# Six of eight pairs of x tiles loaded a second time in transposed form, with the order of the loads around them changed

## The reference, cut to what matters

```
c0 = agg_w(cond) @ x + agg_b(cond)                    # per batch a 64x64 mix of the channels
logits = c0 @ gate_w ; top 2 of 8 experts ; softmax   # gate_w is 1024 x 8
x1 = x + sum over the 2 experts of  w_e * (c0 @ expert_w[e])
c1 = grouped convolution of x1 along the row + context
out = x1 + c1 @ weight.T + rank-16 terms of 2 of 8 experts
```

## Time and profile before

| | |
|---|---|
| median of 3 runs | 867.15 us (867.11 to 867.46) |
| the profiled execution's own time | 865.47 us |
| its span | 863.6 us |
| TensorE busy in the span | 820.6 us (95%) |
| VectorE, ScalarE busy | 400.2 us, 222.9 us |
| queue q1, all loads and stores issued by SP | 90.27 MB, 32.3% of 16 engines' span |
| `res<-in_x` on q1 | 16 transfers of 512 KB, median 14.6 us to landing |
| `work<-in_x_t` on q1 | 3 transfers of 1024 KB, median 7.1 us to landing |
| `c_scratch<-work` on q1 | 16 transfers of 512 KB, median 5.4 us to landing |

### The profile page before, as it was taken

How to read it: one execution, slowest core, us unless ns; L and a number is a source line. 1 busy time by engine, 2 the same in 40 slices (tenths; PEclk the granted TensorE clock), 3 DMA queues, 4 the chain that set the end, 5 groups by cost and what they waited for, 6 DMA issues and landing times.

```text
span 863.6 us, 13175 instructions
## 1 busy us (share of the span) xinstructions
PE 820.6 (95%) x4308; PEld 677.2 (78%) x4309; DVE 400.2 (46%) x920; ACT 222.9 (26%) x347; POOL 89.1 (10%) x137
## 2 busy tenths in 40 slices
PE   5988779999999999999999999999999999999985
PEld 3645468888888888888887888888898889889863
DVE  1376753142333313333133051466666656656597
ACT  2445333242333413333233152310010010001100
POOL 1000021011111011111011012122112111100000
PEclk9999879999999999999999999999999999999999
DMA  8667559656371824727246243684644653521048
GB/s 282 243 198 244 193 203 395 271 178 208 109 268 69 283 97 134 242 81 284 84 164 212 97 167 93 209 251 129 153 108 106 157 125 97 142 77 25 1 133 256
DMA packets 61220, 146.11 MB, mean 169 GB/s; under 512 B 6880, under 2 KB 23536, under 8 KB 60656
## 3 DMA queue, kind: packets, MB, share of 16 engines
q1 hardware_dynamic: 40528, 90.27, 32.3%
q0 software_dynamic: 9968, 36.19, 14.3%
q10 hardware_dynamic: 10704, 19.41, 6.0%
HBM read 97.60 MB, written 39.85 MB: 159 GB/s over the span
## 4 chain that ended last, share of the span: by engine, by line
PE 82%; DMA 7%; DVE 6%; issue 2%; ACT 2%; SPq 1%; DVEq 0%; ACTq 0%; POOL 0%; POOLq 0%
PE bank L1283 62%; PE bank L1322 6%; PE bank L1274 4%; PE bank L1331 4%; DMA c_scratch<-work 2%; PE bank L1182 1%; PE bank L1385 1%; DVE work L1117 1%; PE bank L1145 1%; DMA work<-in_expert_w 1%; PE bank L1230 1%; DMA res<-in_x 1%; DMA work<-y_scratch,pos_c 1%; PE bank L1159 1%; DMA x1p<-res 1%
## 5 line engine op out<-in xcount | busy, mean ns | idle before, releaser
L1283 PE MATMUL bank<-weights,l_hi 128*128 128x512 f32 x1696 | 524.3, 390 | 0.0
L1283 PEld LDWEIGHTS bank<-weights,l_hi 128*128 128x128 f32 x1696 | 319.6, 188 | 64.6
L1283 PE MATMUL bank<-weights,l_lo 128*128 128x512 f32 x848 | 336.2, 396 | 1.4 <-DVE l_lo L906 1.3
L1283 PEld LDWEIGHTS bank<-weights,l_lo 128*128 128x128 f32 x848 | 159.9, 189 | 34.1 <-issue 2.9
L906 DVE TENSOR_TENSOR l_lo<-bank,l_hi 128x512 fp32r<-128x512 f32 x37 | 25.6, 692 | 184.1 <-ACT l_hi L684 184.1
L938 DVE TENSOR_TENSOR weights<-work,weights 128x1024 fp32r<-128x1024 f32 x64 | 76.2, 1223 | 51.7 <-ACT weights L695 51.2
L695 ACT ACTIVATE weights<-work 128x1024 fp32r<-128x1024 f32 x64 | 65.2, 1055 | 43.2 <-DMA work<-in_expert_w 25.1
L540 POOL DMA_INDIRECT work<-c_scratch,idx x37 | 39.9, 1079 | 200.4 <-PE bank L1274 199.3
L1322 PE MATMUL bank<-conv_sb,x1p 128*128 128x128 f32 x512 | 59.8, 275 | 0.6 <-DMA x1p<-res 0.6
L1322 PEld LDWEIGHTS bank<-conv_sb,x1p 128*128 128x128 f32 x512 | 58.8, 192 | 0.9 <-DMA x1p<-res 0.8
L735 ACT ACTIVATE l_hi<-work 128x512 fp32r<-128x512 f32 x32 | 18.4, 623 | 158.1 <-PE bank L1283 157.3
(11 more groups left out here) (174 smaller groups left out, 530.9 us busy)
## 6 DMA issues: line engine op xcount, KB each, us to landing
work<-in_expert_w SPq DMA_DIRECT2D x68, 512.0 KB, 6.4
y_scratch<-work ACTq DMA_DIRECT2D x74, 256.0 KB, 2.1
res<-in_x SPq DMA_DIRECT2D x16, 512.0 KB, 14.6
c_scratch<-work SPq DMA_DIRECT2D x16, 512.0 KB, 5.4
out<-work SPq DMA_DIRECT2D x16, 512.0 KB, 4.2
res<-in_x_ph SPq DMA_DIRECT2D x14, 512.0 KB, 5.5
x1p<-res SPq DMA_DIRECT2D x112, 64.0 KB, 4.7
y_scratch<-ca SPq DMA_DIRECT2D x7, 512.0 KB, 10.1
```

The source lines that it names most:

```text
L1283: mm = pe.matmul(to[:, :], a[:, k, :], b[:, k, cols * HALF:(cols + 1) * HALF], start=(k == 0 and n == 0), stop=(k == HC - 1 and n == 2))
```

## The change

`LOADED` becomes the pairs 2 to 7, so only pairs 0 and 1 are still transposed on the chip, and `x_t` in memory grows from three to six pairs (the host lays it out; no arithmetic). The count of landed `x_t` loads is kept in two semaphores, one for even and one for odd pairs. The four loads of `kern` go behind tile 1. The piece `raw0` that SP asks for at the end of pair `it` is now `it + 1` and waits for `rest0(it - 1)`, where it was `it + 2` and `rest0(it)`. For the last pair, TensorE does `logits` between the first two `mix` products, and `lists(6)` ahead of `ranks(7)`; VectorE does `one_hot(6)` ahead of `route(7)`, and the last two `rest0` ahead of `idx_all`.

```diff
-LOADED = [3, 5, 7]
+LOADED = [2, 3, 4, 5, 6, 7]
@@ semaphores
-        s_xtl = sem("s_xtl")
+        s_xtl = [sem(f"s_xtl_{j}") for j in range(2)]
@@ SP
-            for g in range(QUAD):
-                sp.dma_start(kern_sb[...], kern[g, ...]).then_inc(s_kern, 16)
             load_x(0)
             sp.dma_start(ca[:, mlp:CA_W], consts_a[:, mlp:CA_W]).then_inc(s_const, 16)
             load_x(1)
+            for g in range(QUAD):
+                sp.dma_start(kern_sb[...], kern[g, ...]).then_inc(s_kern, 16)
...
-                    sp.dma_start(row(it % 2 * 2, 2), x_t[tile_rows(n), :]).then_inc(s_xtl, 16)
+                    sp.dma_start(row(it % 2 * 2, 2), x_t[tile_rows(n), :]).then_inc(s_xtl[it % 2], 16)
...
-                if it + 2 < HC:
-                    sp.wait_ge(s_lo, it + 1)
-                    load_raw0(it + 2)
+                if 1 <= it < HC - 1:
+                    sp.wait_ge(s_lo, it)
+                    load_raw0(it + 1)
@@ VectorE, last pair
             take_gate(it)
+            one_hot(it - 1, False)
             route(ch, it)
-            one_hot(it - 1, False)
             place(ch, it)
             one_hot(it, False)
+            for k in range(HC - 2, HC):
+                rest0(k)
             dve.wait_ge(s_list, NT // 2)
             dve.tensor_copy(idx_all[:, :], bank[7][:, 0:P]).then_inc(s_ids, 1)
-            for k in range(HC - 2, HC):
-                rest0(k)
@@ TensorE
-                    pe.wait_ge(s_xtl, 16 * (LOADED.index(it) + 1))
+                    pe.wait_ge(s_xtl[it % 2], 16 * sum(n <= it and n % 2 == it % 2 for n in LOADED))
...
                 mix(it, 0, 0)
+                if last:
+                    logits(it)
                 mix(it, 0, 1)
                 if not last:
                     turn_x(it + 1, 1)
-                logits(it)
+                    logits(it)
...
-                if it > 0 and not last:
+                if it > 0:
                     lists(it - 1, it == 1, False)
...
-            lists(NT // 2 - 2, False, False)
             lists(NT // 2 - 1, False, True)
```

More of the change, by code:

```diff
@@ L397, in load_raw0 @@
                 sp.dma_start(raw0[k % 2], expert_w[0, k, :, :]).then_inc(s_raw0[k % 2], 16)
-            for g in range(QUAD):
-                sp.dma_start(kern_sb[g * QP:g * QP + K8, :, :], kern[g, :, :].rearrange("k (o i) -> k o i", o=QO)).then_inc(s_kern, 16)
             load_x(0)
@@ L403, in _ @@
             load_x(1)
+            for g in range(QUAD):
+                sp.dma_start(kern_sb[g * QP:g * QP + K8, :, :], kern[g, :, :].rearrange("k (o i) -> k o i", o=QO)).then_inc(s_kern, 16)
             for t in range(2, NT):
```

## The result

The changed kernel takes 852.6 us (median of 4 runs, 850.83 to 853.87); its ratio to the kernel before is 0.983 with a 95% interval of 0.9808 to 0.9852, so 12.8 to 16.7 us less, about 14.7. Run again in three later jobs beside the kernel before, the changed kernel had ratios of 0.9811 (0.9782 to 0.9841), 0.9785 (0.9756 to 0.9814) and 0.9817 (0.9786 to 0.9848), so some 16 to 19 us less. A fourth execution of the kernel before took 2739.82 us and is counted nowhere. The profiled execution is the slowest of its four: 853.87 us, span 852.0.

A forecast was written before the change was run, and what follows sets the result against it. TensorE was near full behind the first 113 us; before that, odd pairs stalled above a fixed 7.42 us ring. Gains of 1.73 + 9.76 + 0.45 = 11.9 us gave 855.2 us, range 853.6 to 861.

The forecast's parts named there:

- the start: Up to the first mixes: with kern behind tile 1, the second half's copy comes sooner, a gain of 1.73 us.
- the end: Last pair to first gather: reordered TensorE and VectorE work starts idx_all sooner, a gain of 0.45 us.
- The middle: Pairs 1 to 6: without transposes on the chip each takes 7.42 us, a gain of 9.76 us.
- The bound of 2.04: Upper bound in us on the start's gain, taken as what tile 0 costs now.
- The old sum of 54.28 us: Time from turn_gate of pair 1 to that of pair 7 before, to become 6 x 7.42 = 44.52 us.
- the price of the queue: DMA queue: every pair with an x_t load asks for 8.17 us of transfers in 7.42 us.
- The slack of 3.3 us: Middle pairs: time between a c0 store landing and its buffer being wanted again; it just holds, so the stall counts 0.
- cover enough: x_t loads, asked for nearly two pairs ahead, and raw0, one pair ahead, were said to arrive in time.
- the gather as long as now: End of the stage: the first gather was expected to keep its length in the changed kernel.
- The queue that falls behind: Rival, chance 0.23: transfers make the buffers of c0 set the pace in the pairs, some 3.5 us more, 858.7 us.
- the start unmoved: Rival, chance 0.10: kern loads or constants are what is waited for, so the start gains nothing, 856.9 us.
- the stall in every pair: Rival, chance 0.05: take_c0 behind late stores gives every pair a period of 11.45 us, 879.4 us in all.

The follow-up runs named there:

- kern_first: The changed kernel with the four kern loads back in their old place ahead of tile 0 of x: 855.61 us, ratio 0.9859 to the kernel before.
- more_loads: The changed kernel with 1.15 MB of extra weight loads behind each x_t load: 859.12 us, ratio 0.9868 to the kernel before.
- loads_only: The kernel before with only six pairs loaded transposed and the two semaphores: 866.0 us, ratio 0.9979 to the kernel before.
- old_raw0: The changed kernel with the raw0 requests as before, raw0(it + 2) behind rest0(it): 861.9 us, ratio 0.9921 to the kernel before.
- before_again: The kernel before run again without edit, for a second profile: 870.04 us, ratio 1.0017 to the other runs of itself.

## Why the prediction was right in the middle and too small in the whole

Two terms of the sum failed, both on the low side: the start and the end. The middle held, less what the clock took.

**Start: the term was mis-sized, 3.0 in place of 1.73 us.** The step read ScalarE as free at 9.56 us and let that cap the gain. That time hung on constants that landed at 5.72 us in this one execution and at 4.3 to 4.9 in every other profile. With usual constants, the tile that stood behind `kern` is waited for 3.03 us, and its place gives 3.0 (kern_first). The bound of 2.04, "what tile 0 costs now", was of the same execution and fell with it.

**Middle: right in mechanism.** Six steps of 7.42 us in all profiles of the changed kernel without a clock dip. The old sum of 54.28 us was 53.57 in the second profile of the kernel before, so 9.8 or 9.1 us. What fell was the price of the queue: 8.17 us for a pair's transfers, where the changed kernel has 7.05 us. The busy share alone is no price. Two stretches, the kernel before, 4 us after the queue had started from empty, and more_loads, where it never ran empty:

```profile
50.00:51.00 1.00, 1.00 (x4) 0.40 (x3) 1.00 (x6) 0.00 (x0) 0.00 (x0) 1.00 1.04 221
60.00:76.15 16.15, 14.84 (x97) 9.11 (x93) 13.60 (x68) 6.24 (x9) 0.00 (x0) 1.00 1.02 417
```

Both read as fully busy, and the second moves nearly twice the bytes. Why is not shown. The slack of 3.3 us was not drawn on in the first profile; in the second ScalarE waited 14.6 us for stores and TensorE felt none of it. That it can be used up, more_loads shows. loads_only and old_raw0 show that the loads need the looser order of SP: the argument named both, but the sum gave all 9.76 us to the turning that goes away, and the loads alone brought 3.8 of them in the pairs, or 5.4 without the low clock of that profile's last step. What TensorE then waited for was the `x_t`, for which the prediction had said "cover enough"; with the old requests it is not.

**End: the step failed, 0.45 in place of 2.4 us.** It counted when `idx_all` starts (S + 11.75 forecast, S + 11.37 came) and then took "the gather as long as now". The two `rest0` that it moved had been beside GpSimd's copy and issue, and cost them 1.6 us. The rule that every engine beside a moved instruction is to be read was kept for VectorE and TensorE and not for GpSimd. The other 0.4 us are `place(7)` and `rest0`, a little shorter than counted.

**The clock was not in the sum at all.** Pairs 0 and 1 took 19.54 and 19.81 us in two profiles of the kernel before and 20.33, 16.60, 18.93 and 18.52 of the changed one; the forecast said 17.8. In the profiled execution this took back 2.5 us, which is why its time, 853.87, falls so near to the 853.6 that was forecast for it. That agreement is luck: start and end were 1.4 and 1.9 us too small, the clock cost 2.5, and behind the gather this execution was 1.2 us slower than the first profile before.

**The rivals.** The queue that falls behind, the start unmoved and the stall in every pair did not come. The first is real with more bytes: in more_loads the buffers of c0 hold TensorE for 2.2 us. With the old `raw0` requests pairs lengthen too, but by late `x_t`, not by those buffers. The range ended at 853.6 because start and end were bounded by 0.3 and 0.2 us above their terms, with a microsecond for the runs; both bounds were rows of one execution.

To the gather, in means over two profiles before and four after, the gain is 113.6 - 98.4 = 15.2 us: 3.2 to pair 0, 1.1 in pairs 0 and 1, 7.7 in pairs 2 to 6, 3.2 behind (0.8 of the last are half of the low clock in the last pair of before_again). From there to the end the same profiles have 751.6 and 752.9 us. Whether these 1.3 us are a loss or the spread (750.6 to 755.7 over all kernels) stays open.

## What to carry to other kernels

When a wait holds a DMA-issuing engine, everything it would issue next waits too; here six loads gave nothing that could be told until that one request was loosened. Read the bytes moved beside the busy share before you price a queue: 1.04 busy went with 221 GB/s in one stretch and 1.02 with 417 in another. Read the granted clock beside a lengthened stretch before you give its length to a wait. And before an instruction of VectorE is moved, read GpSimd's lines beside its old and its new place.

## What the runs showed of the hardware beyond what was expected

- The same program's first wide products ran at 2.4 GHz from 26.5 us on in one execution and from 31 us in another, by their durations; the granted clock of the profile reads 1.00 before and after the rise.
- In one of four profiles of the changed kernel the granted clock was 0.50 for 3.4 us in pair 1, while TensorE was at work (so it was in three experiments, where pair 1 took 9.10 to 9.12 us). With the rise this spreads pairs 0 and 1 by 3.7 us. Such stretches came elsewhere too: 3.3 us in the last pair of before_again, 6.6 around that of old_raw0, 3.4 in loads_only, 3.4 in more_loads.
- 128 narrow products (8 rows, 32 columns) take 7.05 us where the transposes around them run at half speed, and 4.14 behind two wide ones; the granted clock is 0.50 again at the end of the latter.
- The four `kern` loads, 8 partitions each, hold the tile behind them by 3 us for 0.26 MB; the queue moved about 100 GB/s at 0.88 busy while they passed, and 221 to 418 GB/s in the other stretches shown with a busy share above 0.9.
